# Four edits to the attention stages of a two-layer transformer kernel: filler matmuls on TensorE, scatter and gather order on GpSimd

## The reference: what is computed

```
x = x + attention0(layernorm(x), ctx, ctx, tau, delta)   # 16 heads of width 16
x = x + ffn0(layernorm(x))     # 64 experts, 8 per token, and a shared expert
x = x + attention1(layernorm(x), ctx, ctx, tau, delta)
x = x + ffn1(layernorm(x))     # 8 experts, 2 per token

scores = (q k^T) * tau + delta;   a = softmax(scores / 4);   out = (a v) Wo^T + bo
coef   = weights of the chosen experts, zero elsewhere
ffn    = sum over experts of  coef * (silu(x Wg) * (x Wu)) Wd
```

## Time and profile before

| What | Value |
|---|---|
| Median of three runs | 1391.05 us (1390.77, 1391.05, 1394.84) |
| The profiled execution: its own time | 1394.84 us |
| Its span, first to last instruction | 1393.2 us |
| TensorE busy | 1262.3 us (91%) |
| VectorE busy | 830.6 us (60%) |
| GpSimd busy | 559.0 us (40%) |
| ScalarE busy | 492.7 us (35%) |
| Mean granted clock of TensorE | 0.938 |

### The profile page before, as it was taken

The page is one execution under the profiler, slowest core; times in us unless marked ns, Lnnn a source line. Parts: engine busy times, 40 slices in busy tenths (PEclk is TensorE's granted clock), DMA queues, the critical chain, the costliest instruction groups (busy, mean ns, idle before and its releaser), DMA issues. The chain is left out here.

```text
span 1393.2 us, 40465 instructions
## 1 busy us (share of the span) xinstructions
PE 1262.3 (91%) x12894; PEld 973.0 (70%) x12895; DVE 830.6 (60%) x2642; ACT 492.7 (35%) x1255; POOL 559.0 (40%) x706
## 2 busy tenths in 40 slices
PE   6999999999768999998669999999999889999995
PEld 3666666666536988887336666656666679999995
DVE  3467777777566666665445676666666454444442
ACT  2554454544402433433124444444444212121211
POOL 2226565564551011001554565665642313333332
PEclk9999999999968999999758997888899989999998
DMA  4335444465516778854222333223221513433423
GB/s 113 113 106 153 132 133 145 126 190 157 170 60 197 199 210 251 241 158 133 63 62 78 89 86 84 76 84 85 76 69 42 199 34 79 118 102 102 140 48 79
DMA packets 115804, 166.65 MB, mean 120 GB/s; under 512 B 26480, under 2 KB 96768, under 8 KB 114672
## 3 DMA queue, kind: packets, MB, share of 16 engines
q0 software_dynamic: 22672, 58.41, 15.8%
q1 hardware_dynamic: 46496, 54.35, 13.5%
q10 hardware_dynamic: 46560, 52.98, 12.0%
HBM read 87.82 MB, written 63.49 MB: 109 GB/s over the span
## 5 line engine op out<-in xcount | busy, mean ns | idle before, releaser
L1047 DVE TENSOR_REDUCE mx<-banks 112x2 f32<-112x750 f32 x256 | 235.6, 935 | 122.4 <-PE banks L627 109.9
L1894 POOL DMA_INDIRECT xs_d<-xns,idx x160 | 155.2, 970 | 177.2 <-PE banks L653 131.2
L1567 ACT ACTIVATE shared_buf<-banks 125x672 f32<-125x672 f32 x256 | 172.9, 727 | 89.3 <-PE banks L653 78.9
L1908 POOL DMA_INDIRECT kept<-y_d,yidx x128 | 125.2, 978 | 139.3 <-issue 86.7
L919 PEld LDWEIGHTS banks<-xT,attn_buf 128*128 128x128 f32 x1364 | 159.7, 195 | 5.1 <-DVE xT L1433 3.6
L919 PE MATMUL banks<-xT,attn_buf 128*128 128x128 f32 x1364 | 160.1, 278 | 3.3 <-DVE xT L1433 3.3
L653 PE MATMUL banks<-attn_buf 18*125 18x112 f32 x3072 | 129.7, 292 | 33.1 <-DVE mx L1047 21.6
L864 PE MATMUL banks<-xT,staged 128*128 128x128 f32 x1064 | 142.8, 277 | 7.0 <-DVE staged L1444 6.5
L653 PEld LDWEIGHTS banks<-attn_buf 18*125 18x125 f32 x3072 | 104.3, 190 | 63.3 <-issue 34.5
L864 PEld LDWEIGHTS banks<-xT,staged 128*128 128x128 f32 x1064 | 129.1, 192 | 12.1 <-DVE xT L1433 8.1
L627 PE MATMUL banks<-attn_buf 17*112 17x375 f32 x1024 | 121.8, 547 | 9.2 <-ACT shared_buf L1567 8.8
(11 more groups left out here) (214 smaller groups left out, 1954.3 us busy)
## 6 DMA issues: line engine op xcount, KB each, us to landing
shared_buf<-xs_d SPq DMA_DIRECT2D x136, 128.0 KB, 2.5
y_d<-shared_buf ACTq DMA_DIRECT2D x132, 128.0 KB, 2.6
ringbuf<-in_we SPq DMA_DIRECT2D x6, 2176.0 KB, 8.3
ringbuf<-in_we POOLq DMA_DIRECT2D x32, 384.0 KB, 4.6
attn_buf<-attn_buf SPq DMA_DIRECT2D x128, 93.8 KB
attn_buf<-in_ctxT ACTq DMA_DIRECT2D x29, 375.0 KB
xs_d<-zrow ACTq DMA_DIRECT2D x16, 512.0 KB
y_d<-zrow ACTq DMA_DIRECT2D x16, 512.0 KB
```

Source lines behind the costliest of these rows:

```text
L1047: dve.tensor_reduce(mx[:, i % 2, 2 * p:2 * p + 2], banks[0:Q, 2 * p:2 * p + 2, 0:S], AX.X, ALU.max).then_inc(s_max, 1)
L1567: act.activation(pT[:, slot:slot + 2, :], banks[0:KT, first_bank:first_bank + 2, 0:ST * Q], ACT.Exp, scale=0.25).then_inc(s_exp, 1)
L1894: pool.indirect_dma_start(xs_d[L.number], bass.IndirectOffsetOnAxis(ap=idx[:, b % 2, k:k + 1], axis=0), rows, None).then_inc(s_scat[b % 2] ...
L1908: pool.indirect_dma_start(yg[:, u, k, :], None, y_d, bass.IndirectOffsetOnAxis(ap=yidx[:, u, k:k + 1], axis=0)).then_inc(s_gat[u][k * 4 // ...
```

## The change

1. In `scores_T` the two filler matmuls in slot 1 of bodies 1 to 15 of layer 0 are gone (30 matmuls in all); those of body 0 stay.
2. FILL grows from 8 to 10 matmuls, writes bank 7 instead of bank 4, and first waits for what holds bank 7: here bo2.
3. On GpSimd in layer 0, one of the three scatters of slot 1 moves ahead to slot 0 (1, 3, 2 in slots 0 to 2 become 2, 2, 2).
4. On GpSimd in layer 1, one of the four gathers of slot 1 moves ahead to slot 0, behind the copy of the row numbers.

```diff
@@ FIRST_JOBS, layer 0
-..., ("ROW1", 0), ("MAX", 0), ("FILL", 8)),
+..., ("ROW1", 0), ("MAX", 0), ("FILL", 10)),
@@ scores_T
                     if isinstance(b, int) and b == 0:
                         idle(FILL_SCORES[l][i], bank[SCORES_T[0]])
-                    elif l == 0 and i == 1:
-                        idle(2, bank[SCORES_T[0]])
                     pe.wait_ge(s_mx[i % 2], n * (16 * NQ // 2) + 16 * (i // 2 + 1))
@@ first
                         elif j == "FILL":
-                            idle(r, bank[SCORES_T[0]])
+                            for sm, v in free[1]:
+                                wait(pe, sm, v)
+                            idle(r, M1)
@@ body0 (GpSimd, layer 0)
                     after_scores(n, 0)
                     if in_layer(b, -3):
-                        scatter(L, n - 3, b - 3, 2, 1)
+                        scatter(L, n - 3, b - 3, 2, 2)
                     after_scores(n, 1)
                     if in_layer(b, -3):
-                        scatter(L, n - 3, b - 3, 3, 3)
+                        scatter(L, n - 3, b - 3, 4, 2)
@@ body1 (GpSimd, layer 1)
                     if in_layer(b, 4):
                         output_row_numbers(b + 4, b % 2)
+                        gather(b + 4, b % 2, 0, 1)
                     after_scores(n, 1)
                     if in_layer(b, 4):
-                        gather(b + 4, b % 2, 0, 4)
+                        gather(b + 4, b % 2, 1, 3)
```

More of the change, by code:

```diff
@@ L318, in build @@
         SP_ATTN, SP_TAB, SP_LATE, SP_PACK, SP_ROWS, SP_LAST, SP_OPEN = (0, 39), (18, 57), 19, 20, 21, (25, 30, 36), 37
-        FIRST_JOBS = ((("K0", 0), ("V2", 0), ("K1", 0), ("XT", 0), ("Q", 0), ("XT", 1), ("V01", 0), ("K0", 1), ("K1", 1), ("ROW0", 0), ("Q", 1), ("BO", 0), ("ROW1", 0), ("MAX", 0), ("FILL", 8)),
+        FIRST_JOBS = ((("K0", 0), ("V2", 0), ("K1", 0), ("XT", 0), ("Q", 0), ("XT", 1), ("V01", 0), ("K0", 1), ("K1", 1), ("ROW0", 0), ("Q", 1), ("BO", 0), ("ROW1", 0), ("MAX", 0), ("FILL", 10)),
                       (("UP3", 0), ("XT", 0), ("Q", 0), ("DOWN3", 0), ("ROW0", 0), ("XT", 1), ("Q", 1), ("ROW1", 0), ("MAX", 0), ("BO", 0)))
```

## The result

| | Before | After |
|---|---|---|
| Median of 20 runs each, same chip | 1396.87 us | 1409.24 us |
| Ratio, 95% interval | | 1.008 [1.0056, 1.0104] |
| Profiled execution: its own time | 1394.84 us | 1418.99 us |
| Its span | 1393.2 us | 1417.3 us |

The change made the kernel slower by 0.8%, where no change was forecast; 1409 us lies above the forecast's range. Not all of the distance to the 1391.5 us forecast is the change: the kernel before has a median of 1396.87 us over 20 runs, where the three that the forecast knew had 1391.05. TensorE's busy time on the page of after answers to the earlier trace rows: it went up by 10 us.

The account below looks back on a forecast made before the run. TensorE, busy 91% of the span, was taken to bound the kernel, trading turns with VectorE in layer 0. Terms -1.7 + 2.3 + 0 + 0 = +0.6 us on 1391.05 gave 1391.5 us, range 1386.5 to 1397.5 (8 in 10).

Parts of the forecast that it names:

- Step 1: Layer 0, slot 1: taking out the 30 fillers gains 1.7 us, VectorE's routing being late next; bounds nothing to 4.3 us.
- the floor: Layer 0: VectorE's OP keeps a gap of 0.24 us behind `sel`, read from body 5, leaving body 6 0.19 us.
- rival A: Layer 0: the fillers kept the clock up; 1.3 us per fall, 1400 us with one every other body; chance 0.14.
- threshold of four falls: Layer 0: clock falls decide from four in 15 bodies on, 5.2 - 0.6 us being over 4.2 us.
- Step 2: Ahead of `scores_T` of body 0: FILL behind bo2 with 10 matmuls costs 2.3 us; ends 2.2 and about 4 us.
- rival D: At FILL: the clock falls in its 2 us pause, term near 4 us, time 1393.3; counted within the forecast's 0.70.
- Step 3: Layer 0, GpSimd: moving the scatter to slot 0 costs 0; ends -0.3 us and +0.6 us.
- Step 4: Layer 1, GpSimd: moving the gather to slot 0 costs 0, as nothing waits for it and 0.8 us is spare.
- rival C: Layer 1: GpSimd sets the pace; 1.25 us gained in some 7 of 11 bodies, 9 us, giving 1382; chance 0.06.
- The sum: Whole kernel: -1.7 + 2.3 + 0 + 0 = +0.6 us on the median 1391.05, 1391.6, rounded 1391.5 us.
- drift of layer 1: Layer 1: its clock falls shift when everything before shifts by a microsecond; some 3 us either side; chance 0.03.
- Rival B: Layer 0: VectorE's waits are used up whole, 4.3 us, and FILL's delay is hidden, giving 1386.8; chance 0.07.

Follow-up runs that it names:

- edit 1 alone: The kernel before with only the 30 filler matmuls in slot 1 of layer 0 taken out; ratio 1.0217, again 1.0142.
- edit 3 alone: The kernel before with only one scatter of layer 0 moved from slot 1 to slot 0; ratio 1.0103, again 1.0075.
- edits 1 and 3: The kernel before with the 30 fillers of layer 0 out and one scatter moved to slot 0; ratio 1.0158.
- edit 4: The kernel before with one gather of layer 1 moved from slot 1 to slot 0; alone, ratio 0.9867.

## Why the prediction was wrong

**Step 1, the fillers: the step that failed.** Its first half was right: 0.3 us earlier `scores_T`, and VectorE's OP 0.25 us behind `sel` (204.28 above), the floor taken from the earlier trace rows. But -1.7 us was the small term. What failed is the sentence that all else in the cycle "follows OP rigidly and moves with it", with the row maximum and `scores_T` of slot 2 in its list. With the fillers out (edit 1 alone) that maximum came a microsecond later in five of nine bodies, 2.60 to 2.65 us behind its score rows for 1.63, TensorE's pause in slot 2 went from 0.3 us to 1.1 to 1.3, the next one in slot 0 from 0.6 to 1.2, and the clock fell behind nine of these ten pauses. Measured: +32.6 us in the stage for -1.7.

So the large term was rival A, at 0.14: the clock. Against A stood that slots 0 and 2 pause without a filler and the clock stays up. That is so for pauses of 0.3 and 0.6 us, and it stayed so in the four bodies of edit 1 alone whose pauses kept that length; the weighing did not ask whether the pauses would keep it. A's price was too low as well: 1.3 us for one K projection at the low clock, but a fall lasts over several pieces of work, and 32.6 us for ten falls and the pauses before them are 3.3 us each. (Its threshold of four falls takes the forecast's +0.6 us for a gain; by its own price three would do, 3.9 + 0.6 = 4.5 us.) The Trainium skill, "TensorE: Matmul & The Clock Gate", in its section on the second HAM failure mode, has short pauses between groups of matmuls, often enough, as a cause of a swinging clock. Edit 1 alone agrees with it, 0.90 for 1.00; the kernel before, with its pauses of 0.3 and 0.6 us in every body, kept 1.00.

Two things stay open. Why the signal of slot 2 comes late once the fillers of slot 1 are gone: it is late where three scatters precede it, which they do in the kernel before too. And how much of the loss is the missing work itself and how much the shifted timing, since in slot 2 no run has the long pause together with the fillers. For slot 1 there is such a pair: with the same late signal, edit 3 alone pauses 0.74 us and has one fall, edits 1 and 3 pause 1.3 to 1.4 us and have seven.

**Step 2, FILL:** a size off, and foreseen. 4.1 us instead of 2.3, at the upper end given (about 4): FILL ran in part at the low clock, rival D.

**Step 3, the scatter:** taken as 0, up to +0.6 us; measured +10 us in layer 0 alone (349.6 and 350.1 for 339.1). The step asked whether GpSimd has time in slot 0. It has. It did not ask what an indirect DMA does to other engines' signals while it is issued. The trace of before had a sign of it: in slot 2 of body 6, behind three scatters, `pv` ends at 172.82 and mT starts a microsecond later:

```profile
172.01 0.81 PE L668 MATMUL banks<-shared_buf,vv 125*17 125x112 f32 x21
...
173.83 0.25 ACT L1574 ACTIVATE mT<-banks 4x112 f32<-4x112 f32 x1 [2.93 <-PE banks L668]
```

TensorE's wait in that slot is for VectorE, so this cost nothing. In slot 1 VectorE and then TensorE do wait: the slot is 0.9 us longer in seven bodies, slot 2 behind it mostly 0.2 to 0.3. With the fillers out the moved scatter costs nothing more in sum (11 us less in layer 0 with edit 1), since it takes away falls.

**Step 4, the gather:** taken as 0; measured 0.9867 alone, rival C's direction, at 0.06. In the profiles on slower chips (those with fillers in layer 1 aside) layer 1 takes a median of 388 us with it and 409 without, 21 us, more than C's 9. The place that C named, GpSimd's normalising, is only part: the low clock's median goes from 123 to 88 us, and 35 us less of it are worth 15 to 17 us, as a microsecond of it does half the work (16.3 us for 37.6 between the changed kernel with and without the fillers).

**The sum**, against medians on slower chips: FILL +4, layer 0 +27 (fillers and scatter, which do not add), layer 1 -21 gives about +10, for +12.4 measured (1409.24 - 1396.87) and +7.8 in the repeat (1418.09 - 1410.25). The forecast had +0.6. What was called drift of layer 1, 3 us, was too small: the profile before has the shortest layer 1 of all eight without edit 4.

**Rival B** fell: FILL's delay was paid in full. **D** held.

## What to carry to other kernels

A filler matmul does two things: it fills a pause, and it moves everything behind it. Before taking one out, ask slot by slot what the other pauses of the body would become, not only the one where it stood, and price a fall of the clock by the whole stretch at the low clock. An instruction's place on an idle engine is not free if it disturbs others while it runs; look in the same trace for a slot where it already stands and compare the signals there. And where a stage's time swings with the clock, one profile is one draw: compare its length over several.

## What the runs showed of the hardware

- On the chips where before takes 1397 to 1410 us, a second indirect DMA behind another on GpSimd goes with late signals of TensorE: mT 0.7 to 1.1 us behind the end of `pv` for 0.22, and the row maximum of slot 1 2.55 to 2.6 us behind the rows' start for 1.33. Light work of the same length in its place does not. On the two chips where before takes 1320 us mT starts 0.22 to 0.26 us behind `pv` (0.43 at most where something stands between two scatters).
- On those slower chips bodies 3 to 11 of layer 0 stayed at the high clock with TensorE's pauses at 0.3 and 0.6 us, and also at 0.74 us. Behind pauses of 1.1 to 1.4 us it fell in most cases (nine of ten with the fillers out alone, five to seven of eight with the scatter moved too).
- The same kernel takes 1397 to 1410 us on chips of the one kind and 1320 on the other, about 6% apart. Where layer 1 is as in before, it takes 396 to 416 us on the first and 346 to 352 on the second.
- An addition of two inputs over 112x336 on GpSimd stretches VectorE's two-input operation from 0.28 to 0.77 us; work on single columns does not.
- Whether a filler pays depends on the chip: in layer 1 two per body, beside edit 4, went with 52 us at the low clock for 92 on the slower kind, and left no gain to be seen on the faster.
